# An attention and routed-FFN block on one core: both layer-norm statistics of the first batch taken first, its tokens' copies moved to ScalarE, a second run of filler matmuls, and batch 0's q and k parts stored in two pieces

## The chip, the cores and the metric

One NeuronCore of a Trainium2 chip runs the whole program. The metric is device time in microseconds, the median over runs of the kernel. TensorE makes matmuls and transposes, VectorE (DVE) and ScalarE (ACT) take results from PSUM, GpSimd (POOL) has no access to PSUM, and SyncE (SP) mostly issues DMAs. All engines run their own instruction streams and meet at semaphores.

## The reference

Four batches of 1024 tokens with 256 features, all f32:

```python
xn = layernorm(x)                        # no scale, no offset
x + attn(xn, Wq, Wk, Wv, Wo) + ffn(xn, ...)

# attn: q, k, v = xn @ W.T, 16 heads of 16; q and k are turned by RoPE;
#       probs = softmax(causal(q @ k.T / 4)); (probs @ v) @ Wo.T
# ffn:  xm = 3-tap mix of xn along the tokens
#       9 paths: (xm @ W1[p] + b1[p]) @ W2[p] + b2[p]
#       per token the path with the largest tanh(xm @ Wo1 + bo1) @ Wo2 + bo2 is kept
#       layernorm(xn + kept path) * gamma + beta
```

## The kernel before, in words

Work is cut by batch (n, 4 of them), by half of the tokens (512 of 1024) and by group of four heads (G, 16 groups in all). A planner writes the order of all engines' work out by hand at build time: `plan()` gives each piece a due time in units of a group, `arrange()` (with the cost tables `PE_US`, `OWN_US`, `DMA_US`, `TAKE_US`) picks the next piece so that TensorE stalls least, and every engine then walks the same list `ORDER` and issues the pieces that are its own. Only the prologue, `prologue()` at lines 128 to 185, is in a fixed order: its items have a due time below zero and are emitted as listed. `Places` gives each PSUM piece one of the banks, and `taker()` (L316) says which engine reads it out; its count is what others wait for.

The prologue for batch 0, group 0, goes:

- *load*: SP loads x in two halves of 512 KB into z (L874), then the tables and 14 weights (L879 to L896). ScalarE's queue loads the identity and wqk (L1095, L1096); ScalarE then writes rows of ones into k_st (`set_ones`, L1100).
- *stats, pow, norm*: VectorE makes the statistics of a half (L1251 to L1256), GpSimd the power -1/2 (L1012), VectorE one Newton step and the normalization in place (L1262 to L1271). Half 0 is done in full, and its tokens are transposed by TensorE (*xnT*, L1502), before VectorE turns to half 1. Chunk 0 of the features (128 of 256) is copied out of PSUM by ScalarE (L1112), chunk 1 by VectorE (L1286).
- *qk*: for each half, q then k, TensorE makes two units, even and odd (L1512, two chunks each, and a chunk in f32 is two passes in the profile). In batch 0 VectorE takes each unit with two products, by cos and by sin (L1296, L1297), and finishes the rope with L1304 and L1305. A projection waits for both chunks of its half.
- *hi, rest, mid_cut, lo*: each rotated half is cut into three bf16 parts. ScalarE cuts hi (L1129) and mid (L1134), VectorE subtracts (L1311) and cuts lo (L1316). `parts` and `turned` have two buffers, so the cuts of half 1 wait for those of half 0.
- *store, fill*: SP stores the three parts of q or k of one half, 768 KB, to a scratch tensor in HBM (L901) once lo is cut; when q and k are both stored, a fill reads them back, nine DMAs (L918, L921), as stacks of 96 rows, k_st and q_st. Group 0 has one fill for each half; all later groups have one in all.
- *v* (L1523), copied out by ScalarE (L1140).
- *max*: bf16 scores of group 0 (L1569), 16 units for half 0, reduced by VectorE (L1392, L1395); from them *cut* (L1402 to L1404), *shift* (TensorE L1578, ScalarE L1158) and *place*, two DMAs that put the shift rows into q_st. Behind the first shift `keep_at_work` (L1649) issues 10 matmuls of the identity with itself (L1657) into the bank of the second score unit; their result is never read.

After the prologue come, interleaved by the planner, the second 32 units of max of group 0, the scores proper (L1588), exponentials (L1172), the products with v (L1607), the FFN, and the pieces of the next batches.

The two waits of `store` and `fill` that the change touches:

```python
sp.wait_ge(lo_cut, NTH["lo", n, qk, half])             # store, before its one DMA
sp.wait_ge(parts_stored[qk][c], 16 * (n + 1))          # fill, for each half and for q and k
act.wait_ge(parts_stored[a][c], 16 * (m + 1))          # cut_hi, before it writes parts again
```

Of the kernel before, what the change touches and what calls it, by code (L numbers as in the profile page):

```python
# [28 lines left out]
HALF = S // 2  # L29
# [97 lines left out]
def prologue():  # L127

    out = []

    def head(*name):
        out.append(name)

    def cut(qk, half, *steps):
        for what in steps:
            head(what, 0, qk, half)

    def project(qk, half):
        for eo in range(2):
            head("qk", 0, qk, eo, half)  # L140
        head("rope", 0, qk, half)

    def turn(half):
        for c in range(NC):
            head("xnT", 0, c, half)

    head("load", 0, 0)
    head("load", 0, 1)
    for half in range(2):
        head("stats", 0, 0, half)  # L150
        head("pow", 0, 0, half)
        head("norm", 0, half)
        if half == 0:
            turn(0)
    project(0, 0)
    cut(0, 0, "hi")
    project(1, 0)
    cut(1, 0, "hi")
    turn(1)
    cut(0, 0, "rest", "mid_cut")  # L160
    cut(1, 0, "rest", "mid_cut")
    cut(0, 0, "lo", "store")
    cut(1, 0, "lo", "store")
    head("fill", 0, 0)
    for i in range(2):
        head("v", 0, i)
    project(0, 1)
    cut(0, 1, "hi")
    project(1, 1)
    cut(1, 1, "hi")  # L170
    cut(0, 1, "rest", "mid_cut")
    cut(1, 1, "rest", "mid_cut")
    cut(0, 1, "lo", "store")
    cut(1, 1, "lo", "store")
    head("fill", 0, 1)
    for i in range(2, 4):
        head("v", 0, i)
    for u in FIRST_UNITS:
        head("max", 0, u)
    head("cut", 0, 0)  # L180
    head("shift", 0, 0)
    head("place", 0, 0)
    head("fill", 1, 0)
    return out
# [130 lines left out]

def taker(name):  # L316
    if name[0] in ("xnT", "attnT"):
        return "act" if name[2] == 0 else "dve"
    if name[0] == "qk":
        return "dve" if rope_on_dve(name[1]) else "act"  # L320
    return "act" if name[0] in BY_ACT else "dve" if name[0] in BY_DVE else None
# [407 lines left out]
def build(nc, x, wqk, wv, wo, mixk, w1, b1, b1_last, w2, bo1, wo2, bo2, gamma, beta,  # L729
          cos_t, sin_t, ident, order, scratch, chosen, out):  # L730
    ctx = ExitStack()
    with ctx:
# [88 lines left out]
        lo_cut = sem("lo_cut")  # L821
# [16 lines left out]
        out_stored = [[sem(f"out_stored{a}{c}") for c in range(2)] for a in range(2)]  # L838
        NWEIGHTS = 14
        NCONSTS = 4  # L840
        IDLE_MATMULS = 10
        FILL_DMAS = 9

        def unit(name):
# [10 lines left out]

        def placed_by_act(G, half):
            return (G, half) == (0, 0)

        def pv_before(G, i):

# [7 lines left out]
        def _(eng):  # L868
# [28 lines left out]

            def store(n, qk, half):
                i = turn_of(n, qk, half) % 2
                sp.wait_ge(lo_cut, NTH["lo", n, qk, half])  # L900
                eng.dma_start(scratch[n, qk].rearrange("a e p t -> p (a e) t")[:, :, half * HALF:(half + 1) * HALF],  # L901
                              parts[:, i, :, :, :].rearrange("p a e t -> p (a e) t")
                              ).then_inc(parts_stored[qk][half], 16)

            def fill(G, half):
                n, g = divmod(G, NG)
                a, e = (half * HALF, (half + 1) * HALF) if G == 0 else (0, S)
                for c in (range(half, half + 1) if G == 0 else range(2)):
                    for qk in range(2):
                        sp.wait_ge(parts_stored[qk][c], 16 * (n + 1))  # L910
                if G >= STACKS:
                    sp.wait_ge(slot_filled, FILLED["S", G - STACKS, NS - 1])
                done = second_filled if half else stack_filled[G % STACKS]
                src = [scratch[n, qk].rearrange("a e (r h) t -> (a e r) h t", h=H)[:, g * GH:(g + 1) * GH, a:e]
                       for qk in range(2)]
                st = k_st[:, G % STACKS, :, a:e]
                for row, first, rows in ((0, 0, 3 * DK), (3 * DK, 0, 2 * DK), (5 * DK, 0, DK)):
                    eng.dma_start(st[row:row + rows], src[1][first:first + rows]).then_inc(done, 16)  # L918
                st = q_st[:, G % STACKS, :, a:e]
                for k, part in enumerate(Q_PARTS):  # L920
                    eng.dma_start(st[k * DK:(k + 1) * DK], src[0][part * DK:(part + 1) * DK]).then_inc(done, 16)  # L921
# [44 lines left out]
            for name in ORDER:  # L966
                what = name[0]
                if what == "load":
                    load(*name[1:])
                    if name == ("load", 0, 1):  # L970
                        load_weights()
                elif what == "store":
                    store(*name[1:])
                elif what == "fill":
                    fill(*name[1:])
                elif what == "keep":
                    keep_onehot(name[1])
                elif what == "spread":
                    spread_mask(*name[1:])
                elif what == "place":  # L980
                    place_shift(*name[1:])
                elif what == "out":
                    store_out(*name[1:])
# [107 lines left out]
        def _(eng):  # L1091
# [31 lines left out]
            def cut_hi(n, qk, half):  # L1123
                k = turn_of(n, qk, half)
                act.wait_ge(*roped(n, qk, half))
                if k >= 2:
                    m, a, c = from_turn(k - 2)
                    act.wait_ge(parts_stored[a][c], 16 * (m + 1))
                nc.scalar.copy(parts[:, k % 2, 0, :, :], turned[:, k % 2, :, :]).then_inc(hi_cut, 1)  # L1129

            def cut_mid(n, qk, half):
# [64 lines left out]
            set_ones(1)  # L1196
            for name in ORDER:
                what = name[0]
                if what == "xnT" and name[2] == 0:
                    copy_xnT(*name[1:])  # L1200
                    if name == ("xnT", 0, 0, 0):
                        set_ones(2)
                elif what == "qk" and not rope_on_dve(name[1]):
                    copy_raw(*name[1:])
                elif what == "hi":
                    cut_hi(*name[1:])
                elif what == "mid_cut":
                    cut_mid(*name[1:])
                elif what == "v":
                    copy_v(*name[1:])  # L1210
                elif what == "early":
                    activate_early(*name[1:])
                elif what == "shift":
                    copy_shift(*name[1:])
                    if placed_by_act(*name[1:]):
                        place_shift(*name[1:])
                elif what == "S":
                    exponentiate(*name[1:])
                elif what == "osum":
                    copy_sums(*name[1:])  # L1220
                elif what == "ynorm":
                    normalize_y(*name[1:])
                elif what == "attnT" and name[2] == 0:
                    copy_attnT(*name[1:])

        @block.vector
        def _(eng):
# [37 lines left out]
                link(nc.vector.tensor_tensor(r, rs[:, half, :], r, ALU.mult))  # L1265

            def normalize(n, half):
                norm_root(n, 0, half)
                for t in range(HT):
                    y = z[:, n % 2, half * HT + t, :]  # L1270
# [48 lines left out]
            def mix(n, k, c):  # L1319
                if k == 0:  # L1320
                    dve.wait_ge(weights_loaded, 16 * NWEIGHTS)
                    dve.wait_ge(pads_set, 1)
                    dve.wait_ge(act_took, TOOK["xnT", n, 0, 1])
                    dve.wait_ge(dve_took, TOOK["xnT", n, 1, 1])
                    if n == 0:
                        dve.wait_ge(consts_set, NCONSTS)
                    else:
# [116 lines left out]
            for name in ORDER:  # L1444
# [4 lines left out]
                    normalize(*name[1:])  # L1449
                elif what == "root":  # L1450
                    second_root(*name[1:])
                elif what == "xnT" and name[2] == 1:
                    copy_xnT(*name[1:])
                elif what == "qk" and rope_on_dve(name[1]):
                    turn_unit(*name[1:])
# [32 lines left out]
        def _(eng):  # L1488
# [16 lines left out]

            def project_qk(c, n, qk, eo, half):
                pe.wait_ge(wqk_loaded, 16)
                pe.wait_ge(act_took, TOOK["xnT", n, 0, half])
                pe.wait_ge(dve_took, TOOK["xnT", n, 1, half])
                ps = begin(("qk", n, qk, eo, half), c)  # L1510
                w = (2 * qk + eo) * P
                return nc.tensor.matmul(ps[:, :], wqk_sb[:, c, w:w + P],  # L1512
# [3 lines left out]
            def project_v(m, n, i):  # L1516
                pe.wait_ge(weights_loaded, 16 * NWEIGHTS)
                pe.wait_ge(act_took, TOOK["xnT", n, 0, i // 2])
                pe.wait_ge(dve_took, TOOK["xnT", n, 1, i // 2])
                ps = begin(("v", n, i), m)  # L1520
                t = 2 * i + m
                for c in range(NC):
# [123 lines left out]
                return nc.tensor.matmul(ps[:, 0:D], attnT[:, c, i * P:(i + 1) * P], wo_sb[:, c, :],  # L1646
                                        start=(c == 0), stop=(c == NC - 1))

            def keep_at_work():  # L1649

                former = PL.before["S", 0, 1]
                pe.wait_ge(act_took if taker(former) == "act" else dve_took, TOOK[former])
                for _ in range(IDLE_MATMULS):
                    nc.tensor.matmul(unit(("S", 0, 1))[:, :], ident_bf[:, :],  # L1657
                                     ident_bf[:, None, :].to_broadcast([P, HALF // P, P]), start=True, stop=True)

            in_parts = {"endproj": end_project, "qk": project_qk, "v": project_v, "early": early, "mid": middle, "paths": paths_out,  # L1660
                        "proj": out_project}
            for name in ORDER:
                what = name[0]
                if what == "part":
# [14 lines left out]
                elif what == "shift":  # L1679
                    turn_shift(*name[1:])  # L1680
                    if name == ("shift", 0, 0):
                        keep_at_work()
                elif what == "S":
                    score(*name[1:])
                elif what == "pv":
# [65 lines left out]
```

## Time and profile before

| | us |
|---|---|
| median of 3 runs | 777.78 (777.35 to 777.78) |
| the profiled execution | 779.82 |
| its span | 778.1 |
| TensorE busy, of the span | 739.4 |
| VectorE busy | 641.7 |
| ScalarE busy | 448.7 |
| GpSimd busy | 288.3 |

The span is the time from the first to the last instruction of the profiled execution; that execution's own time includes what lies around it, 1.7 us. A profile of one execution can differ from the median by some microseconds. Line numbers are those of the kernel before. Busy time of a matmul is modelled at its end, since matmuls are pipelined.

### The profile page before, as it was taken

The numbers are of one execution on the slowest core, as the hardware profiler recorded it, in microseconds if no ns is written. First come the engines' busy times: TensorE is split into PE (matmuls) and PEld (weight loads), VectorE is DVE, ScalarE is ACT, GpSimd is POOL, SyncE is SP. The second block draws the span as 40 slices with busy tenths as digits, with TensorE's granted clock in tenths as the row PEclk, the third lists the DMA queues.
The fourth block names the chain that finished last, engine by engine and source line by source line (L and its number), as shares of the span: only waits on it lengthen the run. The fifth ranks groups of instructions, "written<-read, shape, count | busy, mean of one in ns | idle before, by whom it ended". The sixth has DMA issues, their size and how long they took to land.

```text
span 778.1 us, 12612 instructions
## 1 busy us (share of the span) xinstructions
PE 739.4 (95%) x4426; PEld 371.7 (48%) x4426; DVE 641.7 (82%) x1896; ACT 448.7 (58%) x780; POOL 288.3 (37%) x459
## 2 busy tenths in 40 slices
PE   3969999999999999999999999999999999999997
PEld 2512334354565544345465544445465554355544
DVE  4999899889898789888988789898988678878732
ACT  6332655765655654775646745675656565664673
POOL 2001123990615112893524213596243302130524
PEclk9967999999999999999999999999999999999999
DMA  7269050224613434112651615112570615200103
GB/s 243 96 180 172 16 114 6 69 83 110 109 15 63 102 92 78 53 61 82 113 78 28 137 57 113 32 50 73 123 109 2 123 42 102 45 2 2 29 1 82
DMA packets 40594, 59.98 MB, mean 77 GB/s; under 512 B 4830, under 2 KB 36847, under 8 KB 37651
## 3 DMA queue, kind: packets, MB, share of 16 engines
q1 hardware_dynamic: 36002, 54.38, 29.9%
q0 software_dynamic: 4224, 4.19, 4.2%
q8 instruction: 35, 0.57, 0.3%
q10 hardware_dynamic: 304, 0.60, 0.2%
q14 instruction: 29, 0.23, 0.1%
HBM read 42.04 MB, written 16.85 MB: 76 GB/s over the span
## 4 chain that ended last, share of the span: by engine, by line
PE 71%; DVE 10%; POOL 9%; ACT 5%; DMA 2%; issue 2%; SPq 1%; ACTq 0%; DVEq 0%; POOLq 0%
PE bank L1607 15%; PE bank L1588 14%; PE bank L1569 13%; PE bank L1550 7%; PE bank L1560 6%; PE bank L1635 3%; PE bank L1523 3%; POOL prob L1047 3%; PE bank L1512 2%; POOL raw L1026 2%; ACT prob L1172 2%; DVE piecemax L1395 2%; POOL turned L1024 2%; PE bank L1530 2%; PE bank L1617 2%
## 5 line engine op out<-in xcount | busy, mean ns | idle before, releaser
L1172 ACT ACTIVATE prob<-bank 128x512 f32<-128x512 f32 x576 | 324.6, 597 | 193.2 <-PE bank L1588 190.0
L1392 DVE CUSTOM_DVE_ANT_0 bank<-bank,causal_sb 128x384 f32<-128x384 f32 (+3 forms) x512 | 240.3, 512 | 32.8 <-PE bank L1569 32.0
L1569 PE MATMUL bank<-k_st,q_st 96*128 96x512 bf16 (+3 forms) x768 | 235.3, 337 | 9.6 <-DMA q_st<-scratch 4.8
L1047 POOL TENSOR_SCALAR_AFFINE_SELECT prob<-prob 128x256 f32<-128x256 f32 (+1 forms) x320 | 125.9, 430 | 290.3 <-ACT prob L1172 287.4
L1588 PE MATMUL bank<-q_st,k_st 98*128 98x512 bf16 (+3 forms) x768 | 211.0, 329 | 8.2 <-ACT prob L1172 5.6
L1395 DVE TENSOR_REDUCE piecemax<-bank 128x1 f32<-128x512 f32 x256 | 163.9, 682 | 18.5 <-PE bank L1569 18.1
L1607 PE MATMUL bank<-prob,v_sb 128*17 128x512 f32 (+3 forms) x1536 | 142.8, 492 | 0.0
L1569 PEld LDWEIGHTS bank<-k_st,q_st 96*128 96x128 bf16 x768 | 71.9, 98 | 134.7 <-DVE piecemax L1392 49.4
L1588 PEld LDWEIGHTS bank<-q_st,k_st 98*128 98x128 bf16 x768 | 69.5, 97 | 110.6 <-ACT prob L1172 54.3
L1560 PE MATMUL bank<-w_sb,mid 128*128 128x256 f32 (+1 forms) x320 | 83.7, 383 | 0.0
L1392 DVE DVE_READ_ACCUMULATOR2_ANT piecemax<- 128x1 f32 x512 | 72.0, 141 | 0.0
L1607 PEld LDWEIGHTS bank<-prob,v_sb 128*17 128x17 f32 x1536 | 38.3, 97 | 62.4 <-issue 58.8
L1512 PE MATMUL bank<-xnT,wqk_sb 128*128 128x512 f32 x128 | 65.8, 618 | 1.2 <-DVE xnT L1286 0.9
L1550 PE MATMUL bank<-xm,w_sb 128*128 128x512 f32 x128 | 66.2, 598 | 0.0
L1012 POOL TENSOR_TENSOR rs<-ve,mhalf 128x4 f32<-128x4 f32 x16 | 16.4, 1026 | 133.4 <-DVE ve L1256 133.1
L1560 PEld LDWEIGHTS bank<-w_sb,mid 128*128 128x128 f32 (+1 forms) x320 | 57.2, 190 | 11.7 <-DVE z L1383 1.4
L1158 ACT COPY shiftT<-bank 8x512 bf16<-8x512 bf16 x32 | 18.3, 572 | 59.5 <-PE bank L1578 58.6
L1024 POOL TENSOR_TENSOR turned<-raw,cos_sb 128x512 f32<-128x512 f32 x24 | 33.5, 1394 | 25.4 <-ACT raw L1121 19.5
L1026 POOL TENSOR_TENSOR raw<-raw,sin_sb 128x512 f32<-128x512 f32 x24 | 33.6, 1400 | 0.0
L1523 PE MATMUL bank<-wv_sb,xnT 128*128 128x256 f32 x128 | 32.3, 382 | 0.3 <-DVE raw L1297 0.3
L1058 POOL TENSOR_TENSOR z<-z,gamma_sb 128x512 f32<-128x512 f32 x16 | 22.3, 1391 | 27.0 <-ACT z L1184 27.0
L1512 PEld LDWEIGHTS bank<-xnT,wqk_sb 128*128 128x128 f32 x128 | 23.3, 196 | 18.6 <-issue 10.6
(87 smaller groups left out, 699.4 us busy)
## 6 DMA issues: line engine op xcount, KB each, us to landing
scratch<-parts SPq DMA_DIRECT2D x16, 768.0 KB, 3.8
q_st<-scratch SPq DMA_DIRECT2D x90, 128.0 KB, 6.9
k_st<-scratch SPq DMA_DIRECT2D x15, 384.0 KB, 4.7
z<-in_x SPq DMA_DIRECT2D x8, 512.0 KB, 4.3
mask<-chosen SPq DMA_DIRECT2D x16, 256.0 KB
z<-in_x POOLq DMA_DIRECT2D x8, 512.0 KB, 7.3
k_st<-scratch SPq DMA_DIRECT2D x15, 256.0 KB, 5.3
out<-z SPq DMA_DIRECT2D x7, 512.0 KB, 6.5
```

The source lines that it names most:

```text
L1026: nc.gpsimd.tensor_tensor(r[:, eo, :], r[:, eo, :], half_of(sin_sb, half), ALU.mult).then_inc(turned_pool, 1)
L1047: nc.gpsimd.affine_select(out=d, in_=d, compare_op=ALU.is_ge, fill=0.0, base=0, pattern=pattern, channel_multiplier=-1).then_inc(masked, 1)
L1172: nc.scalar.activation(prob[:, place_of(G, i), :], ps[:, :], ACT.Exp, scale=float(DK) ** -0.5).then_inc(act_took, 1)
L1392: nc.vector.tensor_tensor_reduce(ps, ps, causal_sb[:, HALF - w:HALF], 1.0, NEG, ALU.add, ALU.max, to).then_inc(dve_took, 1)
L1395: nc.vector.tensor_reduce(to, ps, AX.X, ALU.max).then_inc(dve_took, 1)
L1512: return nc.tensor.matmul(ps[:, :], wqk_sb[:, c, w:w + P], xnT[:, c, 1 + half * HALF:1 + (half + 1) * HALF], start=(c == 0), stop=(c == NC ...
L1523: ins = nc.tensor.matmul(ps[:, m * D:(m + 1) * D], xnT[:, c, 1 + t * P:1 + (t + 1) * P], wv_sb[:, c, :], start=(c == 0), stop=(c == NC - 1))
L1550: return nc.tensor.matmul(ps[:, :], w1_sb[:, c, j * P:(j + 1) * P], half_of(xm[:, c, :], half), start=(c == 0), stop=(c == NC - 1))
L1560: ins = nc.tensor.matmul(ps[:, m * D:(m + 1) * D], mid[0:rows, j, t * P:(t + 1) * P], w2_sb[0:rows, j, :], start=(j == 0), stop=(j == NJ - 1))
L1569: nc.tensor.matmul(begin(("max", G, u))[:, 0:w], q_st[0:PARTS, G % STACKS, h, t * P:(t + 1) * P], k_st[0:PARTS, G % STACKS, h, k0:k0 + w], ...
L1588: ins = nc.tensor.matmul(ps[:, c:c + w], k_st[:, G % STACKS, h, kb * P:(kb + 1) * P], q_st[:, G % STACKS, h, q:q + w], start=True, stop=True)
L1607: ins = nc.tensor.matmul(ps[CT * h:CT * h + VW, q - half * HALF:q - half * HALF + w], v_sb[:, n % 2, kb, g * GH + h, :], prob[:, place_of( ...
```

## The change

Five things, in the words of the diff:

1. In the prologue, stats and pow of both halves come first, then norm of both halves, then the transposes of half 0. `normalize` of half 1 of batch 0 waits for xn_ready of half 0, since both use the same small tile rt.
2. All xnT copies of batch 0 are ScalarE's (`taker`), and so is set_ones(2) moved behind the second of them.
3. A q or k projection waits only for its own chunk of xnT (`xnT_copied`); mix and v wait for both as before.
4. `keep_at_work` takes a count and is called a second time, with 14 matmuls, ahead of everything TensorE does. Both calls wait for consts_set >= 2, which the cast of the identity to bf16 gives.
5. For batch 0 the hi and mid parts, 4 of 6 rows, are stored at mid_cut, the lo part at lo. parts_stored then counts two transfers for batch 0, so the waits of `fill` and `cut_hi` go from n + 1 to n + 2.

```diff
@@ prologue
     for half in range(2):
         head("stats", 0, 0, half)
         head("pow", 0, 0, half)
+    for half in range(2):
         head("norm", 0, half)
-        if half == 0:
-            turn(0)
+    turn(0)
@@ taker
     if name[0] in ("xnT", "attnT"):
-        return "act" if name[2] == 0 else "dve"
+        return "act" if name[2] == 0 or name[:2] == ("xnT", 0) else "dve"
@@ build
-        IDLE_MATMULS = 10
+        IDLE_MATMULS, FIRST_MATMULS = 10, 14
...
+        def xnT_copied(n, c, half):
+            return (act_took if taker(("xnT", n, c, half)) == "act" else dve_took), TOOK["xnT", n, c, half]
@@ SP: store, fill
             def store(n, qk, half):
                 i = turn_of(n, qk, half) % 2
+                rows = scratch[n, qk].rearrange("a e p t -> p (a e) t")[:, :, half * HALF:(half + 1) * HALF]
+                mine = parts[:, i, :, :, :].rearrange("p a e t -> p (a e) t")
+                if n == 0:
+                    sp.wait_ge(lo_cut, NTH["lo", n, qk, half])
+                    eng.dma_start(rows[:, 4:6], mine[:, 4:6]).then_inc(parts_stored[qk][half], 16)
+                    return
                 sp.wait_ge(lo_cut, NTH["lo", n, qk, half])
...
+            def store_leading(n, qk, half):
...
+                sp.wait_ge(mid_cut, NTH["mid_cut", n, qk, half])
+                eng.dma_start(rows[:, 0:4], mine[:, 0:4]).then_inc(parts_stored[qk][half], 16)
...
-                        sp.wait_ge(parts_stored[qk][c], 16 * (n + 1))
+                        sp.wait_ge(parts_stored[qk][c], 16 * (n + 2))
...
+                elif what == "mid_cut" and name[1] == 0:
+                    store_leading(*name[1:])
@@ ACT
-                    act.wait_ge(parts_stored[a][c], 16 * (m + 1))
+                    act.wait_ge(parts_stored[a][c], 16 * (m + 2))
...
-                if what == "xnT" and name[2] == 0:
+                if what == "xnT" and taker(name) == "act":
                     copy_xnT(*name[1:])
-                    if name == ("xnT", 0, 0, 0):
+                    if name == ("xnT", 0, 1, 0):
                         set_ones(2)
@@ DVE
             def normalize(n, half):
+                if n == 0 and half:
+                    dve.wait_ge(xn_ready, NTH["norm", n, 0])
                 norm_root(n, 0, half)
...
-                    dve.wait_ge(dve_took, TOOK["xnT", n, 1, 1])
+                    dve.wait_ge(*xnT_copied(n, 1, 1))
...
-                elif what == "xnT" and name[2] == 1:
+                elif what == "xnT" and taker(name) == "dve":
                     copy_xnT(*name[1:])
@@ PE
             def project_qk(c, n, qk, eo, half):
                 pe.wait_ge(wqk_loaded, 16)
-                pe.wait_ge(act_took, TOOK["xnT", n, 0, half])
-                pe.wait_ge(dve_took, TOOK["xnT", n, 1, half])
+                pe.wait_ge(*xnT_copied(n, c, half))
...
-                pe.wait_ge(dve_took, TOOK["xnT", n, 1, i // 2])
+                pe.wait_ge(*xnT_copied(n, 1, i // 2))
...
-            def keep_at_work():
+            def keep_at_work(count):
                 former = PL.before["S", 0, 1]
-                pe.wait_ge(act_took if taker(former) == "act" else dve_took, TOOK[former])
-                for _ in range(IDLE_MATMULS):
+                if count == IDLE_MATMULS:
+                    pe.wait_ge(act_took if taker(former) == "act" else dve_took, TOOK[former])
+                pe.wait_ge(consts_set, 2)
+                for _ in range(count):
                     nc.tensor.matmul(unit(("S", 0, 1))[:, :], ident_bf[:, :],
...
+            keep_at_work(FIRST_MATMULS)
             for name in ORDER:
...
                     if name == ("shift", 0, 0):
-                        keep_at_work()
+                        keep_at_work(IDLE_MATMULS)
```

## Rows read from the trace of the kernel before

**Rows 1.** The page: engines' busy time; the granted clock in 40 slices, tenths.

```profile
PE 739.4 (95%) x4426; PEld 371.7 (48%) x4426; DVE 641.7 (82%) x1896; ACT 448.7 (58%) x780; POOL 288.3 (37%) x459
...
PEclk9967999999999999999999999999999999999999
```

**Rows 2.** The chain that ended last, 0 to 90 us: start us, us, what.

```profile
43.79 6.46 DMA scratch<-parts
...
56.34 0.40 PE bank L1569
```

**Rows 3.** Timeline of VectorE: start us, busy us, instruction, [idle before <-releaser].

```profile
8.76 0.16 DVE L1262 TENSOR_TENSOR rt<-rs 128x4 f32<-128x4 f32 x1 [1.23 <-POOL rs L1012]
...
13.06 0.69 DVE L1286 COPY xnT<-bank 128x512 f32<-128x512 f32 x1 [2.12 <-PE bank L1502]
13.67 1.39 DVE L1251 BATCH_NORM_STATS2 stats<-z 128x6 f32<-128x256 f32 x4
...
15.51 0.17 DVE L1256 TENSOR_SCALAR ve<-mv 128x4 f32<-128x4 f32 x1
...
18.90 0.68 DVE L1296 TENSOR_TENSOR turned<-bank,cos_sb 128x512 f32<-128x512 f32 x1
...
26.35 0.68 DVE L1286 COPY xnT<-bank 128x512 f32<-128x512 f32 x1
...
31.55 0.68 DVE L1296 TENSOR_TENSOR turned<-bank,cos_sb 128x512 f32<-128x512 f32 x1
```

**Rows 4.** The tile z, 0 to 25 us: its two loads, ns min/median/max, first and last start.

```profile
L874 SPq DMA_DIRECT2D z<-in_x x2: 448/476/504, 0.8 to 1.3; - x2
...
DMA to landing us min/median/max: 4.6/5.7/6.9
```

**Rows 5.** Timeline of GpSimd.

```profile
4.05 0.29 POOL L1005 CAST ident_bf<-ident_sb 128x128 bf16<-128x128 f32 x1 [2.13 <-DMA ident_sb<-in_ident]
```

**Rows 6.** Timeline of TensorE, matmuls (PE) and weight loads (PEld).

```profile
11.09 1.94 PE L1502 MATMUL bank<-ident_sb,z 128*128 128x128 f32 x8 [11.09 <-DVE z L1271]
...
16.59 0.34 PEld L1512 LDWEIGHTS bank<-xnT,wqk_sb 128*128 128x128 f32 x1 [0.52 <-issue]
17.45 0.27 PEld L1512 LDWEIGHTS bank<-xnT,wqk_sb 128*128 128x128 f32 x1 [0.52 <-issue]
17.96 0.19 PEld L1512 LDWEIGHTS bank<-xnT,wqk_sb 128*128 128x128 f32 x1 [0.24 <-issue]
...
22.68 1.04 PE L1502 MATMUL bank<-ident_sb,z 128*128 128x128 f32 x8
...
52.28 3.73 PE L1657 MATMUL bank<-ident_bf 128*128 128x512 bf16 x10
```

**Rows 7.** Busy us in stretches: PE, PEld, DVE, ACT, POOL; clock, DMA share, GB/s.

```profile
38.00:41.50 3.50, 0.64 (x3) 0.21 (x2) 3.50 (x5) 2.13 (x3) 0.00 (x0) 1.00 0.84 197
41.50:55.00 13.50, 9.26 (x27) 2.93 (x28) 13.39 (x41) 2.55 (x4) 0.00 (x0) 0.50 0.58 177
55.00:56.00 1.00, 1.00 (x5) 0.20 (x2) 0.52 (x1) 0.00 (x0) 0.00 (x0) 0.92 0.70 165
79.00:80.00 1.00, 0.26 (x3) 0.02 (x1) 1.00 (x5) 0.00 (x0) 0.00 (x0) 1.00 0.02 7
83.00:85.00 2.00, 2.00 (x6) 0.68 (x5) 1.52 (x4) 1.49 (x3) 0.00 (x0) 0.50 0.00 0
280.00:290.00 10.00, 9.98 (x53) 3.58 (x46) 8.56 (x27) 5.78 (x11) 3.22 (x9) 0.83 0.21 60
```

**Rows 8.** Timeline of ScalarE.

```profile
27.42 0.58 ACT L1112 COPY xnT<-bank 128x512 f32<-128x512 f32 x1
28.20 2.18 ACT L1134 CAST parts<-turned 128x1024 bf16<-128x1024 f32 x2 [0.20 <-DVE turned L1311]
```

**Rows 9.** DMA issues in 42.4 to 43.0 and in 43.4 to 44.0 us.

```profile
scratch<-parts SPq DMA_DIRECT2D x1, 768.0 KB, 4.0
...
scratch<-parts SPq DMA_DIRECT2D x1, 768.0 KB, 6.5
```

More of the change, by code:

```diff
@@ L899, in store @@
                 i = turn_of(n, qk, half) % 2
-                sp.wait_ge(lo_cut, NTH["lo", n, qk, half])
-                eng.dma_start(scratch[n, qk].rearrange("a e p t -> p (a e) t")[:, :, half * HALF:(half + 1) * HALF],
-                              parts[:, i, :, :, :].rearrange("p a e t -> p (a e) t")
-                              ).then_inc(parts_stored[qk][half], 16)
+                rows = scratch[n, qk].rearrange("a e p t -> p (a e) t")[:, :, half * HALF:(half + 1) * HALF]
[4 more added lines that the diff above has]
+                    return
+                sp.wait_ge(lo_cut, NTH["lo", n, qk, half])
+                eng.dma_start(rows, mine).then_inc(parts_stored[qk][half], 16)
+            def store_leading(n, qk, half):
+                i = turn_of(n, qk, half) % 2
+                rows = scratch[n, qk].rearrange("a e p t -> p (a e) t")[:, :, half * HALF:(half + 1) * HALF]
+                mine = parts[:, i, :, :, :].rearrange("p a e t -> p (a e) t")
+                sp.wait_ge(mid_cut, NTH["mid_cut", n, qk, half])
+                eng.dma_start(rows[:, 0:4], mine[:, 0:4]).then_inc(parts_stored[qk][half], 16)
             def fill(G, half):
```

## The prediction

> **What bounds the kernel now.** Read the page first: TensorE is busy 95% of the span, and the granted clock dips only in the first tenth and once near 285 us [rows 1]. So from about 80 us on TensorE sets the pace, and a change to the prologue can only move the moment at which this steady stretch begins. The chain of waits over the first 90 us comes next: up to 57 us almost nothing in it is TensorE. It is VectorE, then a 6.46 us store and the fill behind it, ahead of the second batch of maxima at 56.34 [rows 2]. Then VectorE's timeline, read for its gaps. It idles 2.12 us until its xnT copy at 13.06, and a good microsecond at each power; from 18.90 on it runs without a gap worth naming until half 1 is cut [rows 3]. The first projection unit had ended by 17.5 (its last weight load at the slow pitch is at 17.45, the next one 0.51 later), so VectorE was late for it: it was still in norm of half 1 [rows 3, 6]. The last question is how much earlier the block at 18.90 can begin.
>
> The sum is made in the profiled execution (779.82 us, span 778.1), which lies 2.0 us above the 777.78 median of three; I subtract the gain from the median.
>
> **Statistics first.** Stats and powers keep their cost; their order changes. Stats of half 0 start at 5.5, when the first x load has landed (issued at 0.8, 4.6 us [rows 4]), and end at 7.5, at 2.0 us a half (13.67 to 15.68 before [rows 3]). Stats of half 1 need the second x load: issued at about 1.3 and taking 6.9 us, the longer of the two loads, it lands at 8.2. So stats of half 1 run 8.3 to 10.3. Only then comes norm of half 0, 2.2 us (from 8.76 to 0.15 before the first transposes at 11.09 [rows 3, 6]): it now ends at 12.5. The added wait of norm 1 on norm 0 is on VectorE's own finished work: nothing, or 0.1 if the write must drain. The 2.12 us gap is filled, both powers run under other work, and norm 1 ends at 14.7. But the first transposes wait until 12.65 where they began at 11.09: 1.56 later.
>
> **The 14 matmuls.** They start at about 4.45, once ident_bf is cast (GpSimd, 4.05 to 4.34 [rows 5]), and hold nothing up. The clock column reads 1.00 there, before its first record, so durations tell: eight transposes took 1.94 us at 11.09 and 1.04 at 22.68, and projection passes are 0.86 apart up to 17.45 and then 0.51, with the change inside, so 0.43 at twice the clock [rows 6]. TensorE began at the lower level (1.2 GHz) and rose near 17.6. Fourteen at the lower level take 14 x 0.43 = 6.0 us, to 10.4; if the clock rises on the way they end earlier, about 9. Then TensorE idles 2.2 to 3.6 us until 12.65. What happens then decides the result, and the rows speak for a fall: with TensorE idle from 38.64 the clock fell at 41.5; after 79 to 80, busy 0.26 of that microsecond, it was at the lower level by 83 [rows 7]. I take it that the transposes still run at the upper level, and that the clock is down when the projections are under way, from about 14.2.
>
> **ScalarE's copies.** Chunk 0 is transposed by 13.2 and copied 13.3 to 13.9 (0.58 each [rows 8]), chunk 1 13.9 to 14.45. The projection now waits for its own chunk only, so it starts at 14.0 on chunk 0, and the serial second copy hides under its two passes. Before, it started at 13.90. The set_ones piece that moves behind them is hidden as long as it takes less than the 7 us until ScalarE's next job, the hi cut after 21; were it longer, hi would be late by the rest.
>
> **Projections to R (the end of both ropes of half 0).** Unit 1: four passes, 3.4 us at the lower level, minus 0.2 for the start at the upper one: 17.25. A rise follows continuous work by some 3.4 us in one place (the idle matmuls start at 52.28 behind a few transposes, and the clock is up at 55.1) [rows 6, 7], so I take 17.6 again. Units 2 to 4 at 1.72: 19.0, 20.7, 22.4. VectorE: unit 1 17.4 to 18.6, unit 2 19.1 to 20.3, rope to 21.5, unit 3 to 22.7, unit 4 to 23.9, rope to 25.2. Before, R was 26.35 (the start of the second xnT copy) [rows 3]. Gain at R: 1.15.
>
> **The cuts of half 0.** VectorE loses the 0.60 us copy. But ScalarE now makes two copies between hi and mid_cut: hi from R + 0.1, copies from R + 1.05, mid_cut at R + 2.1. Before it started at 28.20, R + 1.85 [rows 8]. VectorE's rest cuts end at R + 2.3, so lo 1 starts about R + 3.2 and the pair ends at R + 5.5, against 5.2 (26.35 to 31.55) [rows 3]. This takes 0.3 back: an engine that was idle becomes the wait. Gain 0.85 when half 1's projections reach VectorE. TensorE is not late there: its units 5 and 6 are made from R + 1.6 on. Half 1 of the prologue keeps its shape (its ACT chain has no xnT copies), so 0.85 stands at the last lo cut and at the end of the first 16 maxima.
>
> **Stores in two parts.** Four more issues on SP, which otherwise sits in waits for the cuts and has the fill of half 0 issued by then: nothing. One 768 KB store alone landed in 4.0 us, the second behind it in 6.5 [rows 9]; both must land before the fill is issued. 512 of 768 KB now leave one lo cut or more earlier. With the first parts leaving some 2.5 us before the last cut ends, the wait behind it falls from 6.5 to between 4.0 (a store alone) and 5. So the fill lands 1.5 to 2.5 us earlier relative to VectorE. That is worth only 0.3: the 10 idle matmuls behind shift, 3.73 us from 52.28, end at 56.01, and TensorE waited from there to 56.34 for the fill [rows 2, 6]. They stay, in front of the maxima, and depend on VectorE's cut. The score units depend on the shift rows' placing, which moves by 0.85 alone. [...]
>
> **Steady stretch.** The order is made by the planner, and its costs change. I worked its prologue: with take 0.55, norm 2.2 and so on, the k lo cut of half 0 moves from 31.02 to 29.02 in its time, and all engines' times after it hang on that, so all move by the same 2.0. The order after the prologue should be unchanged, and the gain passes on: 0.85 to 1.15, less what a fixed moment of the clock's rise takes around 76 us. Sum: 0.9 of gain, 777.78 - 0.9 = 776.9.
>
> **Rivals.** All chances include 0.2% (1.56 us), about what a measurement here can tell from none.
> 1. *Clock stays up* through the 2.2 us gap (18%). Then the projections start at 14.0 at 1.72 a unit: 15.7, 17.4, 19.1, 20.9; VectorE runs 15.85 to 17.05, 17.55 to 18.75, rope to 20.0, and 3.73 more (half of 18.90 to 26.35 [rows 3]): R = 23.75, gain 2.6, less 0.35 for the copies, plus 0.3 for the fill: 2.5, 775.3 us. For it: each idle stretch that preceded a fall was a little longer or repeated. Against: [rows 7]. The Trainium skill, in TensorE: Matmul & The Clock Gate (The HAM clock gate), says that the throttled level is the default and activity releases it; by that rule the 14 matmuls do their work, and this is its result if the gap is not counted.
> 2. *Slower: TensorE becomes the bound of the prologue* (17%). It starts 1.56 later, and before it needed 6.4 us of work (11.09 to 17.5) to see the clock rise. With transposes at the lower level the projection starts at 14.6, and with a rise only near 20.5 units end at 18.0, 20.9, 22.6, 24.3. VectorE: unit 2 to 22.2, rope 23.4, unit 3 24.6, unit 4 25.8, rope 27.1: 0.75 later than 26.35, 1.05 after the copies, 0.75 after the fill: 778.5. It turns slower than before as soon as unit 2 ends after about 20.0.
> 3. *The gain is altered in the steady stretch* (20%): stretches at the lower clock level come at other places. One of some 3.4 us cost 1.7 us near 285 us (0.83 of full over 10 us) with TensorE busy throughout [rows 7]. One fewer gives 775.2, one more 778.6. A tie in the planner that falls the other way is in here too, of unknown sign.
> 4. *The change does nothing* (5%): the second store part or the mask of idle matmuls keeps 56.34 where it is: 777.8.
> The forecast itself has 40%, between 776.3 and 777.6.
>
> **Chances.** Faster by over 0.2% (below 776.2): rival 1, a third or more of rival 3, and the forecast's edge: 0.32. Slower (above 779.3): the upper part of rivals 2 and 3 together: 0.11. Within: 0.57. The range holds rival 1 and rival 2 with a little over: 774.6 to 778.9.
>
> **What would show it.** First transposes at 12.6, not 11.1; their duration (1.0 or 1.9) tells the clock. Projection passes 0.86 apart until 17 mean the forecast, 0.43 from 14.0 rival 1, 0.86 beyond 18 rival 2. VectorE's first product with cos at 17.4 (forecast), 15.9, or 18.1. ScalarE's first mid cut should wait behind two copies, not behind rest. The fill should land before the idle matmuls end, and the first 512-wide maximum start near 55.3. The prediction is wrong if the second x load lands by 7.5, if the fill is still what TensorE waits for, or if the instruction order after 60 us differs.

## The result and the profile after

The changed kernel takes 780.79 us in the median of 8 runs (779.64 to 783.71), against 777.86 in 8 runs of the kernel before (777.35 to 778.53): ratio 1.0042, 95% interval 1.0026 to 1.0057. The forecast was 776.9, with a range of 774.6 to 778.9. The kernel is slower where a small gain was expected, and lies 3.9 us above the forecast. The profiled execution has 783.54 us and a span of 781.8, 3.7 more than the span before, so it lies 2.75 above its median. Three executions whose clock was low from end to end (939.6 us of the kernel before, 941.32 of bridge_k_first, 852.92 of hold_bridge2) are left out of all medians, ranges and ratios below.

The page of the changed kernel, engines' busy time and granted clock, answers to [rows 1]:

```profile
PE 745.6 (95%) x4440; PEld 373.5 (48%) x4440; DVE 641.1 (82%) x1894; ACT 449.6 (58%) x782; POOL 287.6 (37%) x459
...
PEclk9965999999999999999999999999999999999999
```

TensorE is busy 6.2 us longer; the 14 new matmuls alone take 5.89 of that. In the clock one slice differs, the fourth (58.6 to 78.2 us): 5 tenths where it had 7. The chain of the whole run now names a DMA that was not there: `q_st<-shiftT`, 2%.

The timeline of VectorE in the changed kernel (start us, busy us, instruction, [idle before <-releaser]), against [rows 3]:

```profile
7.95 1.41 DVE L1268 BATCH_NORM_STATS2 stats<-z 128x6 f32<-128x256 f32 x4 [0.68 <-DMA z<-in_x]
...
17.38 0.69 DVE L1315 TENSOR_TENSOR turned<-bank,cos_sb 128x512 f32<-128x512 f32 x1 [3.09 <-PE bank L1530]
...
25.28 2.42 DVE L1330 TENSOR_TENSOR turned<-turned,parts 128x1024 f32<-128x1024 f32 x2
28.39 2.36 DVE L1335 TENSOR_TENSOR parts<-turned,parts 128x1024 bf16<-128x1024 f32 x2 [0.69 <-ACT parts L1151]
30.67 0.68 DVE L1315 TENSOR_TENSOR turned<-bank,cos_sb 128x512 f32<-128x512 f32 x1
```

The first product comes at 17.38 (18.90 before), both ropes of half 0 end at 25.28 (26.35), half 1 starts at 30.67 (31.55). The 0.69 us before the lo cut is the wait for ScalarE that its two copies cause. Up to here the change gains 0.88 us, and up to the shift transposes 0.91 (50.85; 51.76 before). Now the timeline of TensorE from there, against [rows 6]:

```profile
4.81 5.89 PE L1677 MATMUL bank<-ident_bf 128*128 128x512 bf16 x14 [4.81 <-POOL ident_bf L1022]
12.23 1.06 PE L1521 MATMUL bank<-ident_sb,z 128*128 128x128 f32 x8 [1.52 <-DVE z L1290]
...
50.85 0.59 PE L1596 MATMUL bank<-ident_bf,shifts 128*8 128x128 bf16 x4 [1.97 <-DVE shifts L1423]
51.37 3.95 PE L1677 MATMUL bank<-ident_bf 128*128 128x512 bf16 x10
55.16 0.38 PE L1587 MATMUL bank<-k_st,q_st 96*128 96x512 bf16 x1
59.42 0.59 PE L1606 MATMUL bank<-q_st,k_st 98*128 98x512 bf16 x1 [3.89 <-DMA q_st<-shiftT]
```

The first 512-wide maximum starts at 55.16, without a wait for the fill: 1.18 us earlier than at 56.34 [rows 2]. Then all is lost at one place. The first score unit, next in TensorE's order, waits 3.89 us for the shift rows in q_st, and behind it stand the maxima that VectorE needs. The chain of the changed kernel from 48 to 62 us (start us, us, what) and SP's timeline say why:

```profile
52.08 1.19 ACTq L1182
...
53.31 5.98 DMA q_st<-shiftT
```

```profile
47.83 1.28 SPq L933 DMA_DIRECT2D k_st<-scratch  x3
49.15 2.78 SPq L936 DMA_DIRECT2D q_st<-scratch  x6
51.98 1.53 SPq L933 DMA_DIRECT2D k_st<-scratch  x3
53.55 3.00 SPq L936 DMA_DIRECT2D q_st<-scratch  x6
```

The earlier stores let the fill of half 1 go out at 47.83 instead of 50.31. What nobody waits for yet, the fill of group 1 (nine transfers, 1.5 MB), is next in SP's queue and goes out at 51.98. Before, it went out at 54.48 (kernel before, SP's timeline):

```profile
54.48 1.60 SPq L918 DMA_DIRECT2D k_st<-scratch  x3
```

The two transfers of the shift rows, 4 KB each, leave ScalarE's queue at 52.08 and 53.31 (52.99 and 54.2 before). Before, the first left 1.5 us and the second 0.3 us ahead of that fill; now both leave behind its first transfer. The second lands 5.98 us after its issue, when SP has issued all nine transfers and begun with the fill of group 2 (from 56.59).

Part of the loss comes with the clock. Stretches of the changed kernel, in the columns of [rows 7]:

```profile
13.70:17.10 3.40, 3.40 (x5) 1.33 (x6) 0.59 (x2) 3.38 (x2) 0.00 (x0) 0.50 0.73 256
55.00:58.00 3.00, 0.54 (x3) 0.04 (x1) 0.69 (x1) 0.00 (x0) 0.00 (x0) 1.00 1.02 187
58.00:60.00 2.00, 0.58 (x2) 0.29 (x3) 0.00 (x0) 0.00 (x0) 0.00 (x0) 0.52 1.12 164
60.00:68.00 8.00, 7.95 (x30) 3.34 (x27) 6.70 (x20) 5.07 (x9) 2.75 (x8) 0.50 1.03 165
72.00:82.00 10.00, 9.75 (x43) 2.57 (x43) 8.72 (x30) 0.24 (x1) 0.00 (x0) 0.50 0.39 101
```

The kernel before has such stretches too, but shorter and later ones:

```profile
65.40:75.60 10.20, 9.70 (x32) 1.92 (x36) 9.63 (x35) 0.17 (x1) 0.41 (x1) 0.50 1.01 156
82.50:85.90 3.40, 3.40 (x9) 1.05 (x8) 2.64 (x8) 2.51 (x5) 0.00 (x0) 0.50 0.00 0
```

TensorE idles through the wait, the clock falls during it, and TensorE works at the lower level from 58 to 68 and 72 to 82: some 20 us, against 13.6 before. The first products with v start at 77.14 (72.68 before), 4.5 later. The wait of 3.9 less the gain of 1.2 makes 2.7 of it; the other 1.8, by subtraction, is put down to the longer time at the lower level; no run separates the two.

### The profile page after: what moved, and what is told of

The parts are those of the page before. It is cut to its first block, busy times and chain, and to the rows that moved or that the text cites. A ratio compares the mean times of both kernels' runs of the same rounds, so it can differ in the third digit from the quotient of the medians.

```text
span 781.8 us, 12644 instructions
## 1 busy us (share of the span) xinstructions
PE 745.6 (95%) x4440; PEld 373.5 (48%) x4440; DVE 641.1 (82%) x1894; ACT 449.6 (58%) x782; POOL 287.6 (37%) x459
## 4 chain that ended last, share of the span: by engine, by line
PE 71%; POOL 9%; DVE 9%; ACT 6%; DMA 3%; issue 2%; SPq 0%; ACTq 0%; DVEq 0%
PE bank L1625 14%; PE bank L1606 14%; PE bank L1587 14%; PE bank L1568 7%; PE bank L1578 6%; PE bank L1530 3%; PE bank L1653 3%; PE bank L1541 3%; POOL prob L1064 3%; ACT prob L1189 2%; POOL raw L1043 2%; DVE bank L1411 2%; POOL turned L1041 2%; PE bank L1548 2%; DMA q_st<-shiftT 2%; PE bank L1635 2%
```

## Experiments

Theory A: the shift rows' small transfers share the DMA engines with the fill of group 1, which the split stores let start too early. Rival B: the loss is the clock's, or that of the matmuls and the new order at the start. The comparisons are of many executions, since one kernel's executions differ by several us; ratios are to the kernel before in the same comparison (its medians 777.92, 778.09 and 778.28).

### hold_fill: the changed kernel, group 1's fill held back

```diff
                 if G >= STACKS:
                     sp.wait_ge(slot_filled, FILLED["S", G - STACKS, NS - 1])
+                if G == 1:
+                    sp.wait_ge(shift_placed[0], 16 * SHIFT)
```

> The changed kernel, with SP made to wait for the two shift-row transfers before it issues the fill of group 1. Theory A (the shift rows' small transfers, 4 KB each, share the DMA engines with the fill of group 1, which the change lets start at 52.0 instead of 54.5 us, and land at 59.3 instead of before 56.6): the first score unit starts by 55.8 us, TensorE has no 3.9 us gap there, and the median is 776.9 us (776.0 to 777.7). Rival B (the loss comes from where the stretches at the lower clock level fall, or from the 14 matmuls and the new order at the start): the gap may go, but the time stays near 780.8, at least above 779.

Measured: 777.58 us median (775.04 to 784.53, 12 runs), ratio 0.9994 (0.9971 to 1.0016). Chain and TensorE's timeline of its profiled execution:

```profile
51.57 1.73 DMA q_st<-shiftT
```

```profile
4.78 4.54 PE L1679 MATMUL bank<-ident_bf 128*128 128x512 bf16 x14 [4.78 <-POOL ident_bf L1024]
12.19 1.06 PE L1523 MATMUL bank<-ident_sb,z 128*128 128x128 f32 x8 [2.87 <-DVE z L1292]
13.58 7.11 PE L1532 MATMUL bank<-xnT,wqk_sb 128*128 128x512 f32 x16 [0.33 <-ACT xnT L1131]
...
53.44 0.38 PE L1608 MATMUL bank<-q_st,k_st 98*128 98x512 bf16 x1
```

Two lines take 3.2 us off the changed kernel: theory A. The second transfer of the shift rows lands 1.73 us after its issue, and the first score unit starts at 53.44 without a wait (1.7 us of its lead come from the clock, which was up for this execution's projections). The median is 0.7 above the 776.9 that was expected, within its range. Against the kernel before no gain is shown: the interval holds 1.

### one_store and split_only: the split taken out, and alone

```diff
 # one_store: the changed kernel, with
-    store_leading(...) at mid_cut, rows 4:6 at lo
+    one dma_start(rows, mine) at lo, and waits for n + 1
 # split_only: the kernel before, with
-    one dma_start(rows, mine) at lo, and waits for n + 1
+    store_leading(...) at mid_cut, rows 4:6 at lo, and waits for n + 2
```

> The changed kernel with each store of batch 0 in one transfer again, issued after lo. Theory A: fill of half 1 and fill of group 1 move back by 1.5 to 2 us against VectorE's work, the shift rows' transfers find the engines as free as in the kernel before, first score unit by 56.0 us, median 777.1 us (776.3 to 778.0). Rival B: still above 779.

> The kernel before with nothing but the stores in two parts. Theory A: fill of half 1 lands some 1.5 us earlier, the fill of group 1 is issued at about 53.0, just when the shift rows are, these land late, and the median is 779.5 us or more (up to 781.5). Rival B: 777.9 (within 0.7 of before), since order, copies and filler matmuls are as before.

Measured: one_store 778.54 us (776.42 to 785.67, 12 runs), 1.0019 (0.9994 to 1.0044). split_only 782.99 us (781.74 to 786.28, 6 runs), 1.0061 (1.0040 to 1.0082). TensorE's timeline of split_only, then of one_store:

```profile
56.07 0.38 PE L1583 MATMUL bank<-k_st,q_st 96*128 96x512 bf16 x1
60.44 0.59 PE L1602 MATMUL bank<-q_st,k_st 98*128 98x512 bf16 x1 [3.98 <-DMA q_st<-shiftT]
```

```profile
55.06 0.39 PE L1573 MATMUL bank<-k_st,q_st 96*128 96x512 bf16 x1 [0.40 <-DMA q_st<-scratch]
55.28 0.38 PE L1592 MATMUL bank<-q_st,k_st 98*128 98x512 bf16 x1
```

With nothing but the stores changed, the wait for the shift rows is there, 3.98 us, and the loss is larger than expected (782.99 against at most 781.5). The rest of the change hides part of it in the profile (the first score unit at 59.42 instead of 60.44); in the medians the intervals of the two ratios overlap. Rival B falls, since order, copies and filler matmuls are those of the kernel before. one_store loses the wait, but its median lies above its range: five of its twelve executions are at 782.4 to 785.7, the others at 776.4 to 778.8.

### one_store_hold: are those five the same race?

```diff
+                if G == 1:
+                    sp.wait_ge(shift_placed[0], 16 * SHIFT)        # in one_store
```

> one_store with SP waiting for the shift rows' transfers ahead of the fill of group 1. The 12 executions of one_store lay in two heaps, 776.4 to 778.8 and 782.4 to 785.7 us. Theory A (the upper heap is the shift rows coming late, by a close race with that fill): no execution above 781, median 777.4 us (776.6 to 778.4). Rival (the upper heap is the clock): the upper heap stays, about 4 in 10.

Measured: 778.00 us (775.65 to 781.99, 12 runs), ratio 1.0002 (0.9988 to 1.0017). The heap above 782 is gone; one execution is at 781.99, above the bound I gave. The race may be the cause of the heap, but this is not shown: the profile of one_store is of an execution from the lower one, and there the shift rows leave 1.48 us ahead of the fill (51.72; 53.20), as in the kernel before (1.49). And hold_fill, which holds the fill back too, has one execution at 784.53. Against hold_fill, the split is worth 0.4 us once the collision is out, about the 0.3 of the prediction, but within the scatter of both.

### before_hold: the control for the wait

```diff
+                if G == 1:
+                    sp.wait_ge(shift_placed[0], 16 * SHIFT)        # in the kernel before
```

> The kernel before with SP waiting for the shift rows' transfers ahead of the fill of group 1: a control for the wait itself. Theory A: the shift rows land at about 56 anyway and the fill of group 1 starts some 1.5 to 2 us later, with time to spare before its first use near 72: 777.8 (777.0 to 778.6). If the fill of group 1 has no time to spare, the kernel is slower by up to 2 us.

Measured: 779.40 us (777.66 to 782.72, 12 runs), ratio 1.0014 (0.9999 to 1.0028): above its range, though not clearly slower. TensorE's timeline of the kernel before, then of before_hold, at the first score unit of half 1:

```profile
80.17 0.60 PE L1588 MATMUL bank<-q_st,k_st 98*128 98x512 bf16 x2 [0.91 <-DMA q_st<-shiftT]
```

```profile
81.20 0.60 PE L1590 MATMUL bank<-q_st,k_st 98*128 98x512 bf16 x2 [1.41 <-DMA q_st<-shiftT]
```

Held back, the fills and loads reach further into the time in which half 1's shift rows are sent: from 78 to 80 us the DMA share is 0.68 and then 0.02 in the kernel before, 1.11 and 0.64 in before_hold. The wait is 0.5 longer. It looks as if holding moves some of the collision to the next transfer; hold_fill shows the same wait at 1.32.

### hold_no_first and hold_bridge: what the matmuls at the start do

```diff
-            keep_at_work(FIRST_MATMULS)                    # hold_no_first, in hold_fill
-        IDLE_MATMULS, FIRST_MATMULS = 10, 14
+        IDLE_MATMULS, FIRST_MATMULS = 10, 24               # hold_bridge, in hold_fill
```

> hold_fill without the 14 matmuls at the start. Theory A (they raise the clock, but it falls again in the idle time before the transposes, except where an execution is lucky): transposes take 1.9 us from 12.2, the first product with cos starts at 17.5 to 18.5 us, the last cut of half 0 and all after it 0.6 to 1 us later than with them; median 778.2 us (777.4 to 779.4), against 777.6 for hold_fill. Rival (the 14 matmuls keep the clock up as meant): first product with cos 2 us later than in hold_fill (15.65) in all executions and the median 2 us above hold_fill.

> hold_fill with 24 instead of 14 matmuls at the start, so that TensorE has work until the first transposes at 12.2. Theory A: the clock is up at 13.6 and stays up, a projection unit takes 1.72 us from the first, the first product with cos starts at 15.7 (up to 16.5 where the 24 end late), the first score unit near 53.5, median 776.4 us (775.5 to 777.6). Rival: the clock falls anyway around 14 and the time is that of hold_fill, 777.6.

Measured: hold_no_first 778.90 us (777.19 to 781.94, 12 runs), ratio 1.0012 (0.9999 to 1.0024). hold_bridge 776.14 us (774.43 to 778.77, 12 runs), ratio 0.9977 (0.9965 to 0.9990). VectorE's first product with cos in the one and the other:

```profile
17.18 0.69 DVE L1317 TENSOR_TENSOR turned<-bank,cos_sb 128x512 f32<-128x512 f32 x1 [2.76 <-PE bank L1532]
```

```profile
15.61 0.69 DVE L1317 TENSOR_TENSOR turned<-bank,cos_sb 128x512 f32<-128x512 f32 x1 [1.40 <-PE bank L1532]
```

With none, 14 and 24 matmuls the medians are 778.9, 777.6 and 776.1; the intervals of none and 24 are apart, that of 14 overlaps both. Fourteen end at 9.3 to 10.7 us and leave 1.5 to 2.9 us idle before the transposes; then it is chance whether the clock is up for the first projection. It was in one of four profiles (hold_fill, up at 13.58; first product at 15.65). In the three others (the changed kernel, one_store, one_store_hold) the product came at 16.8 to 17.4, no earlier than the 17.18 with none, which itself came before the 17.5 that was expected. Twenty-four leave 0 to 0.62 us, and in the four profiles of hold_bridge, bridge_dve, bridge_no_hold and bridge_k_first the first product came at 15.6 to 15.9. hold_bridge is faster than both kernels here; its second comparison is below.

### bridge_dve: one copy back on VectorE

```diff
-        return "act" if name[2] == 0 or name[:2] == ("xnT", 0) else "dve"
+        return "act" if name[2] == 0 or name[:2] == ("xnT", 0) and name[3] == 0 else "dve"
```

> hold_bridge with the copy of chunk 1 of half 1 back on VectorE. Theory A: ScalarE has one copy between hi and mid_cut instead of two, VectorE's wait of 0.69 us before the first lo cut goes and its copy of 0.60 us comes back: the end of the lo cuts of half 0 moves by -0.35 to 0 us, median within 0.4 us of hold_bridge. Rival (two copies on ScalarE are a real gain because they free VectorE): 0.6 us slower than hold_bridge.

Measured: 776.66 us (774.53 to 780.90, 12 runs), ratio 0.9984 (0.9967 to 1.0001). No difference from hold_bridge can be told. In the profiles the wait of 0.69 is gone, the copy is back, and the lo cuts of half 0 start at 26.60 (26.62 in hold_bridge).

### bridge_no_hold and bridge_k_first: none, half or all of the fill beside the small transfers

```diff
-                if G == 1:                                  # bridge_no_hold, in hold_bridge
-                    sp.wait_ge(shift_placed[0], 16 * SHIFT)
 # bridge_k_first, in hold_bridge: the same wait behind the three k transfers
                 for row, first, rows in ((0, 0, 3 * DK), (3 * DK, 0, 2 * DK), (5 * DK, 0, DK)):
                     eng.dma_start(st[row:row + rows], src[1][first:first + rows]).then_inc(done, 16)
+                if G == 1:
+                    sp.wait_ge(shift_placed[0], 16 * SHIFT)
```

> hold_bridge without the wait on SP (so: the changed kernel with 24 matmuls for 14). Theory A: the prologue is as early as in hold_bridge (first product with cos near 15.7), but the fill of group 1 is issued near 50.2 against the shift rows' 50.3, these land near 57.5, the first score unit waits some 4 us, and the median is 779.3 us (778.5 to 780.5), 3 us above hold_bridge. Rival (the clock, not the transfers, made the changed kernel slow): within 1 us of hold_bridge.

> hold_bridge with the wait moved behind the three k transfers (768 KB) of the fill of group 1, so that half of that fill overlaps the shift rows' transfers. Theory A, if the harm grows with the bytes in flight beside the small transfers: these land some 2 us late instead of 4, median 777.8 us (777 to 779), between the two. Rival (the harm is in the count of transfers queued, nine against three, or is all or nothing): as hold_bridge, 776.1, or as bridge_no_hold, 779.3.

Measured: bridge_no_hold 782.74 us (780.89 to 785.47, 6 runs), ratio 1.0057 (1.0036 to 1.0079). bridge_k_first 779.57 us (777.86 to 781.33, 11 runs), ratio 1.0009 (0.9995 to 1.0024). The chain's entry for the second transfer of the shift rows, bridge_k_first, then bridge_no_hold:

```profile
51.82 3.99 DMA q_st<-shiftT
```

```profile
51.96 8.14 DMA q_st<-shiftT
```

SP's timeline of bridge_no_hold:

```profile
49.05 1.35 SPq L933 DMA_DIRECT2D k_st<-scratch  x3
50.45 2.91 SPq L936 DMA_DIRECT2D q_st<-scratch  x6
53.40 1.35 SPq L933 DMA_DIRECT2D k_st<-scratch  x3
```

1.73 us with nothing issued beside it (hold_fill), 3.99 with three transfers and 768 KB, 8.14 with all nine and 1.5 MB and, from 53.40, the fill of group 2: the harm grows with how much goes out beside the small transfer. Bytes and the number of transfers grow together here, so which of them counts is not shown. Both medians are above their ranges (by 0.6 and 2.2 us). In bridge_no_hold the fill went out at 49.05, 1.7 us ahead of the first small transfer, and the first score unit waited 6.19 us where I had priced 4: TensorE's faster start is more than given back, 6.6 us against hold_bridge. The clock in the projections cannot be what made the changed kernel slow, since this one has it up there and is slower still. Behind the wait it is low here too, from 56.5 to 83.8 us.

### hold_bridge2: the better kernel again

No edit: the code of hold_bridge.

> hold_bridge once more, the same code, as the candidate for the better kernel: ratio to the kernel before 0.9977 again, within its interval of 0.9965 to 0.9990, median 776.1 us (775.4 to 776.9).

Measured: ratio 0.9982 (0.9963 to 1.0000), median 777.37 us (775.17 to 780.75, 11 runs) against 778.28 for the kernel before. The ratio is as expected, the median above its range and close to hold_fill's 777.58. The two comparisons put the gain over the kernel before at about 0.2%, 1.5 us; the second alone reaches to no gain.

## Why the prediction was wrong

By its steps:

- **Statistics first**: right. The second x load set the start of stats of half 1 (7.95; 8.3 predicted) and the transposes came at 12.23 (12.65), 1.1 later than before.
- **The 14 matmuls**: right in kind. They took 5.89 us, TensorE idled 1.52 us, the transposes took 1.06 (the upper level), and the clock fell at 13.7. Predicted first product with cos: 17.4; measured 17.38. Rival 1, the clock staying up, is what hold_fill's profile shows (15.65; 15.85 worked out).
- **Projections, cuts**: right. Gain at R 1.07 (1.15), at the start of half 1 0.88 (0.85), and ScalarE's copies became the wait of 0.69.
- **Stores in two parts**: this step failed. The mechanism was right as far as it went: the fill of half 1 goes out 5.0 us after the last cut instead of 6.5, and behind the idle matmuls this is worth 0.3. But I followed the earlier landing only to the one fill that had a reader, and wrote that the shift rows' placing "moves by 0.85 alone". SP's next item, the fill of group 1, moved 2.5 us (54.48 to 51.98), past the issue of the shift rows, which moved 0.91. Its price at the first score unit was 3.89 us, and about 3 us in the median (780.79 against 777.58 with the fill held back). The Trainium skill, in DMA: Bandwidth & Descriptors (Issuing engines are not separate DMA queues), says that transfers started by ScalarE and by SP run on the same 16 engines and interleave. The trace agrees: the small transfers have ScalarE's queue to themselves and still take 1.73 us alone and up to 8.14 beside a fill. By the trace's packet records about half of the added 4.25 us goes before the packets start: the four 1 KB packets of the second transfer start 1.2 to 1.4 us after its issue in hold_fill and 3.3 to 3.8 us after it in the changed kernel, and take 0.1 us or less each in both. The rest passes between them and the landing.
- **Steady stretch**: the planner's order after the prologue is unchanged, as worked out (behind the 14 new ones TensorE's 4426 matmuls come in the same order). The clock took its share, as rival 3 had it: 58 to 68 and 72 to 82 us, against 65.4 to 75.6 and 82.5 to 85.9 before. The fall at 58 came within the idle wait, as it did in split_only (59.2) and bridge_no_hold (56.5), so it goes with the wait; what brought the stretch from 72 to 82 is not shown.
- **The range** had a slower side only from TensorE's clock (rivals 2 and 3). A transfer that nobody waits for was not among the rivals; "what would make it wrong" named the fills' landing, not the shift rows'.
- **The forecast's gain** of 0.9 us is seen in the profile up to the shift transposes (0.91). In the medians it is not shown even without the collision: hold_fill's ratio is 0.9994, and its interval holds both 1 and a gain of 0.9 us.
- **A reading**: the clock's dip near 285 us stands in [rows 7]; the slices of [rows 1] are too coarse to show it.

What stays open: why before_hold is 1.5 us above the kernel before by median. Half 1's shift rows, 0.5 us later, account for a third, and the interval includes 0. Whether the upper heap of one_store was the race is inferred from its going away only. And whether it is the bytes or the number of the bulk transfers that delays the small ones.

## What to carry to other kernels

When a wait gets shorter, read on in the queue of the engine that waited: everything behind it moves too, and what is issued early without a reader can stand in the way of a small transfer that has one. Hold the bulk transfer until the small one has landed, and then look at the next small transfer. Let filler matmuls reach until the real work: with 1.5 to 2.9 us idle behind them their effect was a matter of luck here.

## What the runs showed of the hardware

A 4 KB transfer on ScalarE's queue landed 1.73 us after its issue with the DMA engines nearly idle (share 0.04 from 51.6 to 52 us), 3.99 beside 768 KB, and 5.98, 6.33 (split_only) and 8.14 where SP issued 1.5 MB beside it and began with the next fill before it landed. TensorE's clock fell at 13.7 after an idle stretch of 1.52 us in one execution and held through 2.87 us in another, with the same matmuls around both; the 14 ahead of the stretch took 5.89 us in the first and 4.54 in the second, so the clock rose later in the first. Executions of one kernel scattered by 3.5 to 9.5 us (bridge_k_first 3.5, hold_fill 9.5); the kernel before by 1.2 in its first 8 runs and by 5.3 in 29 later ones.
